# Cross attention pass: layer norm scaling moved from VectorE to ScalarE, key copies and key remainders reordered

## The reference, cut to what matters

```python
def _layernorm(x, axis=-1, eps=1e-05):
    m = jnp.mean(x, axis=axis, keepdims=True)
    v = jnp.var(x, axis=axis, keepdims=True)
    return (x - m) / jnp.sqrt(v + eps)
...
        Q = jnp.einsum('bnd,ed->bne', query, Wq) + bq
        K = jnp.einsum('bnd,ed->bne', key, Wk) + bk
        V = jnp.einsum('bnd,ed->bne', value, Wv) + bv
        scores = (jnp.einsum('bqd,bkd->bqk', Q, K) + score_matrix) / jnp.sqrt(jnp.asarray(D_HEAD, jnp.float32))
        weights = jax.nn.softmax(scores, axis=-1)
        out = jnp.einsum('bqk,bkd->bqd', weights, V)
        return jnp.einsum('bnd,ed->bne', out, Wo) + bo
...
    x = x + _L0_xattn_ref(_layernorm(x, axis=-1), ctx_1024, ctx_1024, fside_BxSxS2_0, ...)
```

## Time and profile before

| | |
|---|---|
| median of 3 runs | 1416.93 us (1416.09 to 1420.04) |
| time of the profiled execution | 1417.16 us |
| its span, first to last instruction | 1415.1 us |
| mean granted TensorE clock | 0.993 of full speed |
| PE busy | 1348.3 us, 95% |
| DVE busy | 1162.6 us, 82% |
| ACT busy | 771.1 us, 54% |
| POOL busy | 632.9 us, 45% |

### The profile page before, as it was taken

One profiled execution on the slowest core, in us unless ns is written; L12 is line 12 of the kernel. 1 busy time (PEld: TensorE's weight loads), 2 busy tenths in 40 slices (PEclk: granted clock), 3 DMA queues, 4 the chain that ended last, 5 costly groups with the idle time before them and its releaser, 6 DMA issues. The chain is left out here.

```text
span 1415.1 us, 19299 instructions
## 1 busy us (share of the span) xinstructions
PE 1348.3 (95%) x6330; PEld 1102.4 (78%) x6330; DVE 1162.6 (82%) x1844; ACT 771.1 (54%) x1493; POOL 632.9 (45%) x526
## 2 busy tenths in 40 slices
PE   5799999999999999999999899999998899999998
PEld 4677788887888878888886788888887687777776
DVE  4999989889898898988988887776675978888874
ACT  5765666656666566666555334344434355555554
POOL 4564344443443434434346334444447344444552
PEclk9999999999999999999999999999999999999999
DMA  9000101001000010010140454444441202222212
GB/s 344 4 21 11 60 31 60 1 30 59 30 30 30 30 59 30 0 60 1 60 156 1 164 224 164 163 163 160 138 162 60 90 30 89 89 89 89 89 60 89
DMA packets 54539, 113.92 MB, mean 81 GB/s; under 512 B 2768, under 2 KB 7120, under 8 KB 52560
## 3 DMA queue, kind: packets, MB, share of 16 engines
q1 hardware_dynamic: 54480, 113.22, 22.6%
HBM read 88.05 MB, written 25.17 MB: 80 GB/s over the span
## 5 line engine op out<-in xcount | busy, mean ns | idle before, releaser
L793 POOL TENSOR_TENSOR a_ss<-a_ss,a_eu 128x512 f32<-128x512 f32 x64 | 82.6, 1291 | 285.1 <-DVE a_ss L609 285.1
L591 DVE SCALAR_TENSOR_TENSOR bank<-bank,k_or_row 128x510 f32<-128x510 f32 x192 | 132.5, 690 | 60.0 <-ACT k_or_row L473 59.3
L798 POOL TENSOR_TENSOR a_sv<-a_sv,a_euv 128x512 f32<-128x512 f32 x64 | 82.5, 1290 | 119.1 <-DVE a_sv L626 119.1
L473 ACT ACTIVATE k_or_row<-bank 128x512 f32<-128x512 f32 x192 | 113.8, 592 | 22.4 <-PE bank L81 18.6
L493 ACT ACTIVATE bank<-bank,a_nbr 128x510 f32<-128x510 f32 x64 | 42.2, 659 | 114.2 <-DVE bank L591 114.2
L380 PE MATMUL bank<-a_wo_hi,a_y_hi 128*128 128x512 f32 x256 | 103.7, 405 | 0.0
L380 PE MATMUL bank<-a_wo_hi,a_y_lo 128*128 128x512 f32 x256 | 100.4, 392 | 0.0
L380 PE MATMUL bank<-a_wo_lo,a_y_hi 128*128 128x512 f32 x256 | 100.2, 391 | 0.0
L802 POOL TENSOR_TENSOR a_y_lo<-a_yy,a_y_hi 128x512 fp32r<-128x512 f32 x64 | 85.2, 1331 | 2.0 <-ACT a_y_hi L516 2.0
L1480 POOL TENSOR_TENSOR b_cx_lo<-b_cx,b_cx_hi 128x512 fp32r<-128x512 f32 x32 | 40.5, 1299 | 99.1 <-ACT b_cx_hi L1172 99.1
L609 DVE TENSOR_TENSOR_SCAN a_ss<-a_mask,a_ee 128x514 f32<-128x514 f32 x64 | 78.6, 1229 | 2.2
(11 more groups left out here) (239 smaller groups left out, 4721.6 us busy)
## 6 DMA issues: line engine op xcount, KB each, us to landing
xres<-in_x SPq DMA_DIRECT2D x8, 1024.0 KB, 5.2
x_after_attention<-xres SPq DMA_DIRECT2D x8, 1024.0 KB, 4.3
xin<-x_after_attention SPq DMA_DIRECT2D x8, 1024.0 KB, 5.5
b_ct<-in_ctx_t SPq DMA_DIRECT2D x8, 1024.0 KB, 4.8
b_cx<-in_ctx SPq DMA_DIRECT2D x8, 1024.0 KB, 7.8
xres<-x_after_attention SPq DMA_DIRECT2D x8, 1024.0 KB, 5.6
x_after_cross<-xres SPq DMA_DIRECT2D x8, 1024.0 KB, 4.4
xin<-x_after_cross SPq DMA_DIRECT2D x8, 1024.0 KB, 5.5
```

Of the source, the lines that this page charges most:

```text
L473: sc.activation(u3[:, :, 1:], ps[m][:, :, :], ACT.Copy, scale=MIX[m]).then_inc(left[m], 1)
L591: ve.scalar_tensor_tensor(out=ps[m][:, :, 0:T - 1], in0=ps[m][:, :, 1:T], scalar=1.0 - MIX[m], in1=u3[:, :, 0:T - 1], op0=ALU.mult, op1=AL ...
L793: gp.tensor_tensor(ss3[:, :, 0:T], ss3[:, :, 0:T], eu[:, :, :], ALU.add).then_inc(b_done, 1)
L798: gp.tensor_tensor(sv3[:, :, 0:T], sv3[:, :, 0:T], euv[:, :, :], ALU.add).then_inc(a_done, 1)
```

## The change

The scaling of the cross pass becomes an activation on ScalarE, `rstd * x + nmr`, where `nmr` is the negated mean times the scale, made by GpSimd with two operations more. In the loop ScalarE scales two blocks between the two probability copies and two behind them; the key copies move right behind the exponentials, around query copies 0 and 1. VectorE does all four statistics ahead of query remainder 0 and the aggregates ahead of remainder 1. GpSimd makes two key remainders before the scale and two after it. In the prologue ScalarE scales tile 0 ahead of the key copies and tile 1 behind query copy 3.

```diff
--- before.py
+++ after.py
@@ -151,6 +151,7 @@
         self.mu_sb = sb("mu_sb", [P, 2, KC])
         self.stats, self.mv = sb("stats", [P, SUB, 6]), sb("mv", [P, SUB, 2])
         self.rstd, self.half, self.eps = sb("rstd", [P, SUB]), sb("half", [P, SUB]), sb("eps", [P, SUB])
+        self.nmr = sb("nmr", [P, SUB])
         self.x1_stored, self.x2_stored = (ctx.enter_context(nc.semaphore(n)) for n in ("x1_stored", "x2_stored"))
 
         self.bank = [ctx.enter_context(nc.psum_tensor(f"bank{j}", [P, N], F32)) for j in range(8)]
@@ -906,7 +907,7 @@
             sem(n) for n in ("st_done", "mv_done", "normed", "rq_made", "rq_moved"))
         veps_done, rstd_done, bo_added, cxlo_done, ctlo_done = (
             sem(n) for n in ("veps_done", "rstd_done", "bo_added", "cxlo_done", "ctlo_done"))
-        fwhi_done = sem("fwhi_done")
+        fwhi_done, nmean_done, rstd_made = sem("fwhi_done"), sem("nmean_done"), sem("rstd_made")
 
         def is_second(i):
             return isinstance(i, int) and i == 1
@@ -1152,6 +1153,12 @@
         def _(act):
             sc = nc.scalar
 
+            def normalise(i, subs):
+                wait(act, rstd_done, i + 1)
+                for s in subs:
+                    sc.activation(xin[:, s, :], xin[:, s, :], ACT.Identity, bias=sh.nmr[:, s:s + 1],
+                                  scale=rstd[:, s:s + 1]).then_inc(normed, 1)
+
             def x_high(i, k):
                 wait(act, turned, i * KC + k + 1)
                 sc.activation(xt_hi[:, k, :], turn_bank(i, k)[:, :], ACT.Copy).then_inc(xhi_done, 1)
@@ -1215,6 +1222,7 @@
 
             for n in range(KC):
                 fold_high(n)
+            normalise(0, range(SUB))
             for k in range(KC):
                 context_high(0, k)
             for k in range(KC):
@@ -1224,6 +1232,7 @@
             for c in range(KC):
                 q_high(0, c)
                 context_high2(0, c)
+            normalise(1, range(SUB))
             for k in range(KC):
                 x_high(1, k)
 
@@ -1233,17 +1242,20 @@
                 for s in range(SUB):
                     exponent(i, s)
                 if ahead:
+                    context_high(i + 1, 0)
+                    context_high(i + 1, 1)
                     q_high(i + 1, 0)
+                    context_high(i + 1, 2)
+                    context_high(i + 1, 3)
                     q_high(i + 1, 1)
                 probs_high(i, 0)
+                if ahead:
+                    normalise(i + 2, (0, 1))
                 probs_high(i, 1)
                 if ahead:
-                    context_high(i + 1, 0)
+                    normalise(i + 2, (2, 3))
                     q_high(i + 1, 2)
-                    context_high(i + 1, 1)
-                    context_high(i + 1, 2)
                     q_high(i + 1, 3)
-                    context_high(i + 1, 3)
                 for c in range(KC):
                     pc_high(i, c)
                     if not ahead and c == 1:
@@ -1339,12 +1351,6 @@
                 for s in range(SUB):
                     ve.bn_aggr(mv[:, s, :], stats[:, s, :]).then_inc(mv_done, 1)
 
-            def normalise(i):
-                wait(dve, rstd_done, i + 1)
-                for s in range(SUB):
-                    ve.tensor_scalar(xin[:, s, :], xin[:, s, :], mv[:, s, 0:1], rstd[:, s:s + 1],
-                                     ALU.subtract, ALU.mult).then_inc(normed, 1)
-
             def row_products(i, subs=range(SUB)):
 
                 for s in subs:
@@ -1391,7 +1397,6 @@
             aggregate()
             for n in range(KC):
                 fold_rest(n)
-            normalise(0)
             row_products(0)
             for k in range(KC):
                 x_rest(0, k)
@@ -1406,7 +1411,6 @@
             aggregate()
             q_rest(0, 2)
             q_rest(0, 3)
-            normalise(1)
             row_products(1, (0, 1))
 
             def body(i):
@@ -1422,12 +1426,11 @@
                         x_rest(1, 3)
                 if ahead:
                     move_rq(i + 1)
-                    statistics(i + 2, (0, 1))
+                    statistics(i + 2)
+                    dve.wait_ge(st_done, i * SUB + 3 * SUB)
                     q_rest(i + 1, 0)
-                    statistics(i + 2, (2, 3))
-                    dve.wait_ge(st_done, i * SUB + 3 * SUB)
+                    aggregate()
                     q_rest(i + 1, 1)
-                    aggregate()
                 inverse(i)
                 probs_rest(i, 0)
                 probs_rest(i, 1)
@@ -1436,8 +1439,6 @@
                     q_rest(i + 1, 3)
                 for c in range(KC):
                     pc_rest(i, c)
-                    if c == 0 and ahead:
-                        normalise(i + 2)
                     if c == 1 and two_ahead:
                         row_products(i + 2)
                     if c >= 2 and two_ahead:
@@ -1467,8 +1468,12 @@
                 wait(pool, mv_done, i * SUB + SUB)
                 wait(pool, normed, i * SUB)
                 gp.tensor_tensor(rstd[:, :], mv[:, :, 1], eps[:, :], ALU.add).then_inc(veps_done, 1)
+                gp.tensor_scalar(sh.nmr[:, :], mv[:, :, 0], -1.0, None, ALU.mult).then_inc(nmean_done, 1)
                 wait(pool, veps_done, i + 1)
-                gp.tensor_tensor(rstd[:, :], rstd[:, :], half[:, :], ALU.pow).then_inc(rstd_done, 1)
+                gp.tensor_tensor(rstd[:, :], rstd[:, :], half[:, :], ALU.pow).then_inc(rstd_made, 1)
+                wait(pool, nmean_done, i + 1)
+                wait(pool, rstd_made, i + 1)
+                gp.tensor_tensor(sh.nmr[:, :], sh.nmr[:, :], rstd[:, :], ALU.mult).then_inc(rstd_done, 1)
 
             def context_rest(i, k):
                 wait(pool, cthi_done, i * KC + k + 1)
@@ -1506,9 +1511,11 @@
 
             def body(i):
                 if not is_last(i):
+                    context_rest(i + 1, 0)
+                    context_rest(i + 1, 1)
                     rstd_of(i + 2)
-                    for k in range(KC):
-                        context_rest(i + 1, k)
+                    context_rest(i + 1, 2)
+                    context_rest(i + 1, 3)
                 add_bias(i)
                 if not is_last(i):
                     for s in range(SUB):
```

## The result

The median fell from 1417.18 us (1416.09 to 1420.87, 13 runs) to **1413.66 us** (1411.59 to 1415.48, 13 runs), a ratio of 0.9971 with a 95% interval of 0.9964 to 0.9979. That is 0.29% less, 4.1 us by the ratio. I had forecast 1417.9, one microsecond slower than the 1416.93 known then, and a range of 1411.5 to 1422.5. The result lies inside the range and just inside the 0.3% that I called no change. Its sign is not the forecast's, though, and a ratio of 1 lies outside its interval.

What follows compares the result with a forecast made beforehand. TensorE was taken as the bound. Tile 0 adds 0.4 + 1.9 us, the loop tiles take off 0.8 and tile 6 0.5: +1.0 us on the median of 1416.93, so 1417.9 us, range 1411.5 to 1422.5.

Steps and rivals of the forecast that it cites:

- The steady tile: Loop tiles 1 to 5: the transposes' wait goes, a 1.33 us wait at context chunk 0 comes; each gains 0.17 us.
- Tile 6: Tile 6 of the cross pass, which has no transposes: old idle 0.4 + 1.75, new 1.7, gain 0.5 us.
- Tile 0 gives this back: Tile 0: key copies ahead of query copy 0 wait for their load; it ends 0.4 us late despite the prologue's gain.
- The clock: Tile 0: the 4.3 us wait lowers TensorE's clock, worth 3.4 us, of which 1.9 is added to the sum.
- The hole: Tile 0, before query 2: TensorE is ready at 821.9 but starts at 826.15, 4.3 us idle.
- How much of the low clock lies on the path: Tile 0: of 3.4 us clock loss, 1.7 lie in the wait before context chunk 0; the rest is charged as 1.9.
- How much sooner the keys' load is issued: Tile 0: the load of tile 1's keys is issued at 816.0 instead of 819.90, with 3.9 us taken.
- VectorE's 5.76 us fall away and win no more than that: Loop tiles: relieving VectorE wins only 0.17 us each, since the row on ScalarE holds up another user of TensorE's banks.
- 1, no clock fall: Tile 0: TensorE's clock stays full after the wait, so the same walk without 1.9 us gives 1416.0; chance 0.27.
- 2, no new wait: Loop tiles and tile 6: query remainder 2 comes in time for context chunk 0, 1405.4 us, or 1411 for half; chance 0.12.
- 3, GpSimd late: Seven tiles: GpSimd's power runs long beside VectorE, context chunk 0 is 0.8 us later in each, 1423.5 us; chance 0.14.
- 4, it does nothing: Whole change: TensorE's order hides both placements of the scaling; called excluded, and given no chance of its own.

Runs made afterwards that it cites:

- late: The changed kernel with its 16-byte buffer allocated last in the cross pass, so other buffers start where they did before: 1414.98 us, 0.9986 of before.
- query_first: The changed kernel with ScalarE's query copies 2 and 3 each ahead of the scaling that held it up: 1404.83 us, 0.9912 of before.
- place: The kernel before plus only the unused 16-byte buffer, allocated where the change has it: 1416.53 us, 0.9987 of before.
- keys_only: The kernel before with the change's early key copies, statistics and GpSimd order, scaling left on VectorE, no new buffer: 1412.86 us, 0.9964 of before.
- tile0_keys_late: The changed kernel with tile 0's key copies on ScalarE put behind query copies 0 and 1 and probability copy 0: 1414.44 us, 0.9976 of before.

## Why the prediction went wrong

**The steady tile was right.** The transposes' wait gone, a wait on query remainder 2 at context chunk 0 in its place (forecast 1.33, found 1.26 of idle and 1.42 between the possible and the real start), ScalarE waiting 1.1 on GpSimd (1.26), scalings at 0.71 pitch (two in 1.52): each came out. The net gain per loop tile was forecast at 0.17; the order of work alone (`late`) gave 38.02 - 37.94 = 0.08, 0.4 in five tiles instead of 0.8. `query_first` confirms the mechanism, since moving the copies that cause that wait gives 8.8 us.

**Tile 6** gave 0.75 instead of 0.5.

**The step that failed, first: "Tile 0 gives this back", and with it "The clock".** I summed +0.4 and +1.9 there. The hole itself was forecast at 4.3 and was 4.08; the keys were forecast for 823.6 and ScalarE had them at 823.25; query 2 was forecast for 826.15 and started at 825.88; the clock fell, as counted. But the stretch up to tile 1 came out at +0.47 (changed) and -0.41 (`late`), not at +2.3. Two terms were mis-sized:

- *How much of the low clock lies on the path*: charged 1.9, found 0.9 and 0. The fall itself was as large as I had taken it from another place of the trace: 10 x 0.28 + 10 x 0.06 = 3.4 us in the two windows, which is 6.8 us at the low clock. But the matmuls were slow only from 825.88 to 831.17, so by these windows some 1.5 us of it lay in the hole, where nothing ran. Query products 2 and 3 took 833.97 - 825.88 = 8.09 us instead of 24 x 0.23 = 5.5, so 2.6 were lost. At the full clock they would have ended at 831.4, and context chunk 0 would have stood waiting for query remainder 2, which ended at 833.03. So 1.7 of the loss lay in a wait that was due anyway, as forecast, and 0.9 was left. In `late` the clock over 820 to 830 was 0.83, chunk 0 still waited 0.19 us, and nothing was left.
- *How much sooner the keys' load is issued*: forecast 3.9, found 4.7. It was issued 815.47 - 782.54 = 32.93 us after the start of the pass, before the change 819.90 - 782.29 = 37.61. It follows the last row product of tile 1; the last two of these started at 813.33 and 814.22 and took 0.75 us each, and the one that GpSimd slowed was tile 0's, at 790.90. Counted from the start of the pass, the keys, query 2 and query remainder 2 come 0.5 to 0.6 us sooner than forecast by that. SP's timeline has the load:

```profile
815.47 0.50 SPq L948 DMA_DIRECT2D b_ct<-in_ctx_t  x1
```

The two terms account for the miss. At context chunk 0 the forecast stood 2.7 us behind before; the changed kernel stood 1.1 behind and `late` 0.2. From there to tile 1 both won back 0.6, where I had 0.4.

**Second, a term that the sum did not have.** The change adds a 16-byte buffer, and I gave its placement no line at all, not even one at zero. It is worth 2.0 us in the traces and 1.8 (0.3 to 3.4) by the timed ratio of `place`. Nothing in the trace of before could have given its size, but the diff showed that buffers move, and TensorE reads them: it belonged into the bounds from both sides.

**The sum, put right.** Forecast +1.0. Tile 0 takes off 2.7 (from +2.3 to -0.4), the loop tiles add 0.4, tile 6 takes off 0.25: -1.55 for the order of work, and -2.0 for the buffers make -3.6 us. Timed, the order alone (`late`) is -2.0 (-3.1 to -0.7), the buffers alone (`place`) -1.8 (-3.4 to -0.3), and the whole change -4.1 (-5.1 to -3.0). The terms agree within these intervals.

**One sentence was wrong though the sum did not need it**: "VectorE's 5.76 us fall away and win no more than that: the same row moved to ScalarE holds up another user". The first half takes 5.76 us as the price of the scaling. I had noted that the bias addition moves to about 983, and did not follow that it then leaves VectorE alone; `keys_only` shows the row at 2.37 without any move.

**The rivals.** 1, no clock fall: wrong, the clock was 0.72 over ten microseconds, although its time (1416.0) was nearer. 2, no new wait: wrong, the wait came; its price was near to what `query_first` then won, in part by luck. 3, GpSimd late: wrong, the chain took 1.77 us in the tile shown, and the power 1.03 to 1.06 us in all nine of its executions between 780 and 1110 us. 4, it does nothing: wrong, the prologue, tile 0, the loop tiles and tile 6 all changed.

## What to carry to other kernels

Before a slow row is moved to another engine, look at what runs beside it: a change of order that ends the overlap may bring the whole gain, and the move then only loads another queue. When work is put into an engine's queue, walk that queue to the next instruction whose bank TensorE wants back, and put that one first; here this order was worth 8.4 to 8.8 us, and in the loop the move itself almost nothing. A change that adds a buffer needs a control that adds the buffer alone, and a loss of clock is to be charged only beyond the next wait that would end later anyway.

## What the runs showed of the hardware that was not expected

- **VectorE beside GpSimd.** Four scalings of 128x512 took 5.76 us beside four additions of GpSimd and 2.37 where only the first of them met an addition (1.00 us, the others 0.53). The row product does the same in the prologue of the changed kernel, where GpSimd begins to split keys beside the last of four (VectorE's timeline):

```profile
789.99 0.75 DVE L1360 CUSTOM_DVE_ANT_0 b_row_product<-xin,k_or_row,bqk 128x512 f32<-128x512 f32 x1
790.90 1.81 DVE L1360 CUSTOM_DVE_ANT_0 b_row_product<-xin,k_or_row,bqk 128x512 f32<-128x512 f32 x1
```

  The largest one is in tile 7 of both kernels, one subtraction of 5.46 us in before, beside four additions of GpSimd (5.06 us from 1096.36; VectorE's timeline of before):

```profile
1096.50 5.46 DVE L1370 TENSOR_TENSOR c_diff<-c_xt 128x512 f32<-128x512 f32 x1 [1.64 <-POOL c_xt L1522]
```

- **Where buffers start.** The same matmul over the same sizes took 399 or 390 ns by a shift of 16 bytes in the buffers, and 36.967 us a tile became 36.753; 64 bytes gave 395 ns and 36.890.
- **The granted clock at similar waits.** In `place`, with the schedule of before, TensorE waited 1.83 us before query 2 and the clock over 820 to 830 was 0.88, though the wait of 1.70 in the earlier trace rows had left it at 1.00. Its stretch up to tile 1 was 72.39 us against 69.86:

```profile
820.00:830.00 10.00, 8.16 (x35) 6.47 (x35) 8.40 (x24) 4.57 (x11) 0.73 (x2) 0.88 0.93 377
830.00:840.00 10.00, 9.86 (x53) 8.41 (x52) 5.51 (x7) 4.14 (x7) 8.82 (x8) 0.95 0.98 370
```

  By the two windows the clock accounts for 10 x 0.12 + 10 x 0.05 = 1.7 of the 2.5 us; in the rest is a wait of 1.02 us before the first transpose of tile 2, which before did not have in this tile. So of waits of nearly the same length one went with a loss of 1.7 us and the other with none, and the 2.29 of `tile0_keys_late` left the clock at 1.00. With the 2.16 us at the end of the pass this is the spread of some 2 us that single executions of this kernel have.
